# Second attention of a two-layer kernel: rotary sum ahead of the division, logits read inside the sum of gathered rows, row scaling behind the second gather

## Chip, cores and metric

The kernel runs on one core of one Trainium2 chip. The metric is the device time of one execution in microseconds (us), the median over several runs. The engines are called by the names of the profile: PE is TensorE's matmul side, PEld its weight loads, DVE is VectorE, ACT is ScalarE, POOL is GpSimd, SP is SyncE, which here only issues DMAs.

## What is computed

128 sequences of 64 tokens, 128 features, go through two layers. Each layer is an attention over a context and then a mixture of experts. The change lies in the attention of the second layer, which turns queries and keys by a position (rotary) before the scores:

```python
x = x + _L0_xattn_ref(_layernorm(x), ctx_1024, ctx_1024, mask, ...)
x = x + _L0_ffn_ref(_layernorm(x), ...)          # 32 experts, 4 per token
# second attention, 16 heads of 8
Q, K, V = query @ Wq + bq, key @ Wk + bk, value @ Wv + bv
Q = Q * cos + _rotate_half(Q) * sin
K = K * cos + _rotate_half(K) * sin
attn = softmax(Q K^T / sqrt(8));  context = attn @ V
x = x + context @ Wo + bo
x = x + _L1_ffn_ref(_layernorm(x), ...)          # 8 experts, 2 per token
```

The output of the first layer's experts is in DRAM, one row per token and expert. The second attention begins by gathering four rows per token and adding them to x.

## The kernel before

The residual X stays in SBUF. The program is a chain of stages: attention, slot table, experts, and the same again. Within a stage each engine has its own hand-written instruction list, and semaphores tie the lists together. There is no scheduler; the order of an engine's work is the order of the code.

The attention works in 32 rounds (ITERS), each on two tiles of 128 tokens. A round of an engine is software-pipelined: in round i it works on several pairs of tiles at different depths, and `on(k)` says whether pair i+k exists. For the second attention (`layer` = 1) the rounds are these.

- DVE, `body_with_sums`: the four row maxima of the scores of pair i (`score_unit`, L593); the division of the attention output of pair i-1 by its denominators (`divide`: reciprocal L633, product L635); the rotary step of pair i+1 (`weigh`, L641, twice for cos and twice for sin, the second behind semaphore `rot_psum`, then the sum L652, called `rotate`), which frees semaphore `rope`; the sum of the gathered rows of pair i+3 (`combine`: L571 and L573 fold four rows into one, L576 adds it to X); the copy of the router's logits of pair i-3 out of PSUM (`read_logits`, L608); statistics (L539); the addition of the projected output (`add_output`, L657); the choice of the experts (L621, L625); means and variances (L555, L561, L562), which free semaphore `offsets`.
- POOL, `body_with_gathers`: eight indirect DMAs (`gather`, L419, two tiles times four rows k = 0 to 3) for pair i+4, and `scale_both` (power L437, product L440), which turns the variances of the DVE round before into row scalings. `gather` for k = 0 waits for the first addition of `combine` two pairs earlier (semaphore `row_sum`), since the gathered rows lie in two buffers. `scale_both` waits for `offsets` and frees `scaled_both`.
- ACT, `body_with_spreads`: copies the transposed inputs (L828), places the values (L768), normalises rows with the scalings of `scale_both` (L787, L814), keeps the chosen experts (L752, L753), copies the maxima (L823), copies the transposed expert rows (L759), spreads keys over heads (L742, waits for `rope`), four exponentials (L725), spreads queries (L742).
- PE, `body_with_rotation`: scores (L907), values (L963) and denominators (L969) of pair i-1, four pairs of projections (L989, L990; the second two write the turned operands into bank M_), transposed maxima (L918), transposed scores (L932, L944), transposed expert rows of pair i-3 (L1019, waits for `rot`, since it writes bank M_), next values (L997), router (L1031), output projection (L1006, L1010, waits for the division and for the logits copy, since it writes the same bank), next inputs (L982, L984).

`hold` waits for a semaphore and puts a no-op behind the wait. In the loop the order of DVE is written out as

```python
if on(-1): divide(pv)
if on(1):  ... weigh(nx, QKe, P_, bq, bk, cos, "qk"); rotate(nx)
if on(3):  combine(i.at(3))
if on(-3): read_logits(p3)
```

Of the kernel before, what the change touches and what calls it, by code (L numbers as in the profile page):

```python
# [96 lines left out]
def hold(eng, sem, value):  # L97

    eng.wait_ge(sem, value)
    eng.nop(nofuse=True)  # L100


def build(nc, a, out, ts, ys, yt, bias_parts):

    with ExitStack() as ctx:
# [206 lines left out]
        def attention(layer):  # L312
# [32 lines left out]
            def tiles(buf, i):  # L345
                return buf[:, bass.ds(i.n * 2, 2), :]
# [20 lines left out]
            with nc.Block() as block:  # L367
# [43 lines left out]
                def _(pool):  # L411
                    def gather(i, k):

                        if k == 0 and i.n >= 2:

                            hold(pool, s["row_sum"], i.n * 2 - 3)
                        for j in range(2):
                            at, to = i.n * 2 + j, (j * K0 + k) * D
                            nc.gpsimd.indirect_dma_start(  # L419
                                out=gb[i.par][:, to:to + D], out_offset=None, in_=ys,  # L420
                                in_offset=bass.IndirectOffsetOnAxis(ap=slot[:, at, k:k + 1], axis=0),
                            ).then_inc(gathered[i.par], 16)
# [10 lines left out]
                    def scale_both(i, cols):  # L433

                        q = 1 - i.par
                        pool.wait_ge(s["offsets"], i.n + 4)
                        nc.gpsimd.tensor_tensor(small["rs"][q][:, cols], small["ve"][q][:, cols], power[:, cols], ALU.pow  # L437
                                                ).then_inc(s["rstd_both"], 1)
                        pool.wait_ge(s["rstd_both"], i.n + 4)
                        nc.gpsimd.tensor_tensor(small["mm"][q][:, cols], small["rs"][q][:, cols], small["nm"][q][:, cols],  # L440
                                                ALU.mult).then_inc(s["scaled_both"], 1)
# [61 lines left out]
                    def body_with_gathers(i, on):  # L503
                        if on(4):
                            gather(i.at(4), 0)
                        if (on(-2) or on(2)) and i.n > -2:
                            scale_both(i.at(-1), slice(0 if on(-2) else 2, 4 if on(2) else 2))
                        if on(4):
                            gather(i.at(4), 1)
                        if i.n == -3:  # L510
                            scale_both(i, slice(2, 4))
                        if on(4):
                            gather(i.at(4), 2)
                            gather(i.at(4), 3)
# [9 lines left out]
                def _(dve):  # L524
# [11 lines left out]
                    def tile_stats(i, st, done):  # L536

                        for j in range(2):
                            nc.vector.bn_stats(st[i.par][:, 6 * j:6 * j + 6],  # L539
                                               X[:, bass.ds(i.n * 2 + j, 1), :].rearrange("p i d -> p (i d)")  # L540
                                               ).then_inc(s[done], 1)
# [20 lines left out]
                        nc.vector.tensor_scalar(small["ve"][1 - q][:, cols], moments[:, cols, 1], EPS, None, ALU.add  # L562
                                                ).then_inc(s["offsets"], 1)

                    def combine(i):

                        q = i.par
                        hold(dve, gathered[q], (i.half + 1) * 16 * 2 * K0)
                        of = gb[q].rearrange("p (i h f) -> p i h f", i=2, h=2)
                        two = rows_sum.rearrange("p (i f) -> p i f", i=2)  # L570
                        nc.vector.tensor_tensor(two, of[:, :, 0, :], of[:, :, 1, :], ALU.add).then_inc(s["row_sum"], 1)  # L571
                        hold(dve, s["row_sum"], i.n * 2 + 1)
                        nc.vector.tensor_tensor(two[:, :, 0:D], two[:, :, 0:D], two[:, :, D:2 * D], ALU.add  # L573
                                                ).then_inc(s["row_sum"], 1)
                        hold(dve, s["row_sum"], i.n * 2 + 2)
                        nc.vector.tensor_tensor(tiles(X, i), tiles(X, i), two[:, :, 0:D], ALU.add  # L576
                                                ).then_inc(s["combined"], 1)
# [24 lines left out]
                    def read_logits(i):  # L602
                        dve.wait_ge(s["gate_psum"], i.g + 1)
                        src = R_[:, 2 * D:2 * D + 2 * n_e].rearrange("p (i e) -> p i e", i=2)
                        q = i.par
                        dst = lg[q][:, 0:2 * n_e].rearrange("p (i e) -> p i e", i=2)
                        if layer:
                            nc.vector.tensor_copy(dst, src).then_inc(s["logits"], 1)  # L608
                        else:
                            nc.vector.tensor_tensor(dst, src, gate_b[:].unsqueeze(1).broadcast_to([P, 2, E0]),  # L610
                                                    ALU.add).then_inc(s["logits"], 1)
# [17 lines left out]
                    def divide(i):  # L629

                        q = i.par
                        dve.wait_ge(s["o_psum"], i.g + 1)
                        nc.vector.reciprocal(rec, O_[:, 2 * D:4 * D]).then_inc(s["o_recip"], 1)  # L633
                        dve.wait_ge(s["o_recip"], i.g + 1)
                        nc.vector.tensor_tensor(aoT[q], O_[:, 0:2 * D], rec, ALU.mult).then_inc(s["o_normed"], 1)  # L635

                    def weigh(i, buf, src, b0, b1, tab, done):

                        for h, b in ((0, b0), (1, b1)):
                            at = slice(h * 2 * D, (h + 1) * 2 * D)  # L640
                            last = nc.vector.scalar_tensor_tensor(  # L641
                                buf[:, at].rearrange("p (b s) -> p b s", s=S),
                                src[:, at].rearrange("p (b s) -> p b s", s=S), b,
                                tab[:].unsqueeze(1).broadcast_to([P, 4, S]), ALU.add, ALU.mult)
                        last.then_inc(s[done], 1)

                    def rotate(i):

                        dve.wait_ge(s["rot_psum"], i.n + 1)
                        weigh(i, QKr, M_, bias_t[:, 4:5], bias_t[:, 5:6], sin, "rot")  # L650
                        dve.wait_ge(s["rot"], i.n + 1)
                        nc.vector.tensor_tensor(QKs[i.par], QKe, QKr, ALU.add).then_inc(s["rope"], 1)  # L652
# [33 lines left out]
                    def body_with_sums(i, on):  # L686
                        nx, pv, p3 = i.at(1), i.at(-1), i.at(-3)
                        if on(0):
                            for r in range(UNITS):
                                score_unit(i, r)  # L690
                        if on(-1):
                            divide(pv)
                        if on(1):
                            dve.wait_ge(s["qk_psum"], nx.g + 1)
                            if not (isinstance(nx.n, int) and nx.n < 1):

                                dve.wait_ge(s["rope"], nx.n)
                            weigh(nx, QKe, P_, bq, bk, cos, "qk")
                            rotate(nx)
                        if on(3):  # L700
                            combine(i.at(3))
                        if on(-3):
                            read_logits(p3)
                        if on(3):
                            hold(dve, s["combined"], i.at(3).n + 1)
                            tile_stats(i.at(3), small["st_a"], "stats_a")
                        if on(-1):
                            add_output(pv)
                        if on(-3):
                            choose(p3)  # L710
                        if on(-1):
                            hold(dve, s["added"], pv.g + 1)
                            tile_stats(pv, small["st_r"], "stats_r")
                        if on(3) or on(-1):
                            moments_of_both(i, on(-1), on(3))
# [820 lines left out]
        def gather(pool, n, XE, arrived):  # L1536
            R = len(XE)
            for c in range(GROUP):
                nc.gpsimd.indirect_dma_start(  # L1539
                    out=XE[n % R][:, c * ROW:(c + 1) * ROW], out_offset=None, in_=ts,  # L1540
                    in_offset=bass.IndirectOffsetOnAxis(ap=token_of_slot[:, n * GROUP + c:n * GROUP + c + 1], axis=0),
                ).then_inc(arrived[n % R], 16)
# [472 lines left out]
```

## Time and profile before

| what | value |
|---|---|
| runs | 1750.91, 1751.86, 1755.05 us, median 1751.86 |
| profiled execution | 1748.74 us, span 1746.9 us |
| granted TensorE clock, mean of the span | 0.92 |
| PE, DVE, ACT, POOL busy share | 79%, 67%, 55%, 62% |
| second attention | about 841 to 1294 us of the span |

The stage of the change is a quarter of the span. Its first score reduction starts at 880.53 us. A row of a timeline reads: start in us from the span's start, duration in us, engine, line, operation, output<-input, count of merged instructions, and in brackets the engine's idle time before it with what ended it. Lines are those of the kernel before. A granted clock of 1.00 is 2.4 GHz, 0.50 is 1.2 GHz.

### The profile page before, as it was taken

Reading aid. Unit: us, or ns where it says so; the run is one execution under the profiler, and the core shown is the slowest. Engines: PE = TensorE matmul, PEld = TensorE weight load, DVE = VectorE, ACT = ScalarE, POOL = GpSimd, SP = SyncE. Lnnn points to the kernel's source line nnn. Section 1 sums busy time; section 2 is a strip of 40 time slices with the busy share of each in tenths; the row PEclk is TensorE's granted clock in tenths of the full one; section 3 lists DMA queues with packets and bytes.
Section 4 is the critical chain, followed back from the end, with each engine's and each line's share of the span. In section 5 each row is a group of like instructions: output and inputs, shape, how many; then the busy total and the mean of one; then the engine's idle time right before and its main releaser. Section 6 shows DMA issues by size and latency. Waiting matters only on the chain. (4 is left out here: it accounts for less than half of the span.)

```text
span 1746.9 us, 56992 instructions
## 1 busy us (share of the span) xinstructions
PE 1372.5 (79%) x20302; PEld 1064.4 (61%) x20303; DVE 1176.1 (67%) x3431; ACT 957.2 (55%) x2418; POOL 1091.4 (62%) x1338
## 2 busy tenths in 40 slices
PE   5999999739677777777268888888854799999784
PEld 3677777514377767767156666666632578777663
DVE  5788888689577777777268888888869222322165
ACT  2677777617454545545067676777735344444332
POOL 3777777500377777776577777777210777777773
PEclk9999999959899999999688999999975899999987
DMA  4211111000144444443242222222100111111174
GB/s 161 89 45 36 45 36 46 21 7 1 26 109 105 108 103 109 106 106 104 64 158 66 63 63 62 61 63 59 33 14 1 51 54 55 54 54 54 55 231 136
DMA packets 136994, 122.85 MB, mean 70 GB/s; under 512 B 27675, under 2 KB 121915, under 8 KB 136123
## 3 DMA queue, kind: packets, MB, share of 16 engines
q0 software_dynamic: 26624, 56.35, 12.7%
q1 hardware_dynamic: 110078, 64.47, 12.1%
q8 instruction: 66, 1.08, 0.3%
q10 hardware_dynamic: 192, 0.67, 0.1%
q14 instruction: 34, 0.28, 0.1%
HBM read 80.24 MB, written 41.18 MB: 70 GB/s over the span
## 5 line engine op out<-in xcount | busy, mean ns | idle before, releaser
L1539 POOL DMA_INDIRECT arena<-expert_rows,token_of_slot x432 | 416.0, 963 | 283.8 <-issue 221.9
L419 POOL DMA_INDIRECT arena<-slot_results,slot x256 | 250.3, 978 | 95.7 <-issue 73.6
L1930 DVE TENSOR_TENSOR arena<-bank,arena 128x352 f32<-128x352 f32 x144 | 75.5, 524 | 222.6 <-ACT arena L1909 222.6
L1863 PE MATMUL bank<-W,arena 128*128 x576 | 198.7, 469 | 0.9 <-ACT arena L1921 0.9
L593 DVE TENSOR_REDUCE mx<-bank 128x8 f32<-128x512 f32 x256 | 158.4, 681 | 33.1 <-PE bank L907 31.9
L1774 POOL DMA_INDIRECT token_results<-arena,slot x144 | 141.2, 980 | 53.3 <-issue 43.7
L445 POOL TENSOR_TENSOR arena<-arena,fixed 128x1024 f32<-128x1024 f32 x64 | 121.3, 1916 | 44.6 <-ACT arena L733 44.6
L725 ACT ACTIVATE arena<-bank 128x512 f32<-128x512 f32 x256 | 131.3, 598 | 25.0 <-PE bank L944 25.0
L1637 PE MATMUL bank<-arena 128*128 128x128 f32 x1152 | 144.0, 279 | 0.0
L1877 PEld LDWEIGHTS bank<-W,arena 128*128 128x128 f32 (+1 forms) x864 | 115.5, 192 | 38.2 <-issue 30.8
L1637 PEld LDWEIGHTS bank<-arena 128*128 128x128 f32 x1152 | 136.9, 195 | 0.2
L1582 PE MATMUL bank<-fixed,arena 128*128 128x128 f32 x288 | 48.0, 290 | 101.9 <-DMA arena<-expert_rows,token_of_slot 101.9
L1877 PE MATMUL bank<-W,arena 128*128 (+1 forms) x864 | 121.5, 277 | 1.8 <-ACT arena L1916 1.8
L1863 PEld LDWEIGHTS bank<-W,arena 128*128 128x128 f32 x576 | 100.3, 194 | 33.4 <-issue 3.8
L1732 DVE TENSOR_SCALAR arena<-bank,arena 128x128 f32<-128x128 f32 x288 | 99.0, 344 | 30.7 <-PE bank L1637 30.5
L1909 ACT ACTIVATE arena<-bank 128x352 f32<-128x352 f32 x144 | 66.7, 463 | 94.9 <-PE bank L1863 94.9
L1467 PE MATMUL bank<-arena 128*128 128x288 f16 (+1 forms) x384 | 86.1, 394 | 39.7 <-DVE arena L1406 21.3
L633 DVE RECIPROCAL arena<-bank 128x256 f32<-128x256 f32 x64 | 111.9, 1749 | 4.3 <-PE bank L969 4.0
L742 ACT ACTIVATE arena<-arena,fixed 128x256 f32<-128x256 f32 x256 | 108.8, 508 | 4.2 <-DVE arena L652 4.2
L907 PE MATMUL bank<-arena 32*64 32x256 f32 x2048 | 83.7, 439 | 32.6 <-ACT arena L725 32.1
L1693 ACT ACTIVATE arena<-bank,fixed 128x512 f32<-128x512 f32 x72 | 49.5, 687 | 107.4 <-PE bank L1582 107.4
L1915 ACT ACTIVATE arena<-bank 128x256 f32<-128x256 f32 x144 | 55.2, 383 | 90.5 <-PE bank L1888 90.5
(220 smaller groups left out, 3379.0 us busy)
## 6 DMA issues: line engine op xcount, KB each, us to landing
slot_results<-arena SPq DMA_DIRECT2D x72, 256.0 KB, 2.4
arena<-in_ctx SPq DMA_DIRECT2D x64, 128.0 KB
expert_rows<-arena SPq DMA_DIRECT2D x64, 128.0 KB
arena<-token_results SPq DMA_DIRECT2D x32, 256.0 KB, 3.8
arena<-expert_rows,token_of_slot POOLq DMA_INDIRECT x432, 2.6
W<-in_w SPq DMA_DIRECT2D x4, 1032.0 KB, 5.1
X<-in_x SPq DMA_DIRECT2D x32, 128.0 KB, 2.2
arena<-slot_results,slot POOLq DMA_INDIRECT x256
```

The source lines that it names most:

```text
L419: nc.gpsimd.indirect_dma_start(out=gb[i.par][:, to:to + D], out_offset=None, in_=ys, in_offset=bass.IndirectOffsetOnAxis(ap=slot[:, at, k: ...
L445: nc.gpsimd.tensor_tensor(dst[i.par].rearrange("p (b j k) -> p b j k", b=4, j=4), src[i.par].rearrange("p (b k) -> p b k", b=4).unsqueeze( ...
L593: nc.vector.tensor_reduce(mx[:].rearrange("p (w c) -> p w c", w=2)[:, :, 32 * r:32 * r + 4], U_[r][:, :].rearrange("p (w j k) -> p w j k", ...
L633: nc.vector.reciprocal(rec, O_[:, 2 * D:4 * D]).then_inc(s["o_recip"], 1)
L725: nc.scalar.activation(Pt[r], U_[r][:, :], ACT.Exp, scale=SCALE).then_inc(s["probs"], 1)
L742: last = nc.scalar.activation(dst[i.par].rearrange("p (b j k) -> p b j k", b=4, j=4)[:, :, j, :], src[i.par].rearrange("p (b k) -> p b k", ...
L1539: nc.gpsimd.indirect_dma_start(out=XE[n % R][:, c * ROW:(c + 1) * ROW], out_offset=None, in_=ts, in_offset=bass.IndirectOffsetOnAxis(ap=to ...
L1637: last = nc.tensor.matmul(H_[2 * i.par + half][:, at:at + P], Wc[i.par][:, c * W1_0 + u * F0:c * W1_0 + (u + 1) * F0], XT[i.par][:, c * P: ...
L1732: nc.vector.tensor_scalar(GL[i.par][:, at], h[:, c, 0, :], Wc[i.par][:, b:b + 1], LIMIT, ALU.add, ALU.min)
L1774: nc.gpsimd.indirect_dma_start(out=yt[half], out_offset=bass.IndirectOffsetOnAxis(ap=row_of_slot[:, at:at + 1], axis=0), in_=YE[n % 4][:, ...
L1863: last = nc.tensor.matmul(H_[2 * r + u][:, 0:F1], XT[i.par][:, c * P:(c + 1) * P], W1a[:, bass.ds(x_e, 1), u * F1:(u + 1) * F1], start=Tru ...
L1877: last = nc.tensor.matmul(Y_[j.par][:, d * P:(d + 1) * P], AT[d % 2][0:f, k * P:(k + 1) * P], W1b[0:f, bass.ds(x_e, 1), k * P:(k + 1) * P] ...
```

## The change

Three edits, all in the second attention. On DVE the rotary step of the next pair goes ahead of the division of the last. In `combine` the copy of the logits goes between the second and the third addition; it is still done by itself where there is nothing to combine. On POOL the gather for k = 1 goes ahead of `scale_both`. What is computed stays the same, and so does the number of instructions.

```diff
@@ -503,10 +503,10 @@
                     def body_with_gathers(i, on):
                         if on(4):
                             gather(i.at(4), 0)
+                        if on(4):
+                            gather(i.at(4), 1)
                         if (on(-2) or on(2)) and i.n > -2:
                             scale_both(i.at(-1), slice(0 if on(-2) else 2, 4 if on(2) else 2))
-                        if on(4):
-                            gather(i.at(4), 1)
                         if i.n == -3:
                             scale_both(i, slice(2, 4))
                         if on(4):
@@ -562,7 +562,7 @@
                         nc.vector.tensor_scalar(small["ve"][1 - q][:, cols], moments[:, cols, 1], EPS, None, ALU.add
                                                 ).then_inc(s["offsets"], 1)
 
-                    def combine(i):
+                    def combine(i, logits_of):
 
                         q = i.par
                         hold(dve, gathered[q], (i.half + 1) * 16 * 2 * K0)
@@ -572,6 +572,8 @@
                         hold(dve, s["row_sum"], i.n * 2 + 1)
                         nc.vector.tensor_tensor(two[:, :, 0:D], two[:, :, 0:D], two[:, :, D:2 * D], ALU.add
                                                 ).then_inc(s["row_sum"], 1)
+                        if logits_of is not None:
+                            read_logits(logits_of)
                         hold(dve, s["row_sum"], i.n * 2 + 2)
                         nc.vector.tensor_tensor(tiles(X, i), tiles(X, i), two[:, :, 0:D], ALU.add
                                                 ).then_inc(s["combined"], 1)
@@ -688,8 +690,6 @@
                         if on(0):
                             for r in range(UNITS):
                                 score_unit(i, r)
-                        if on(-1):
-                            divide(pv)
                         if on(1):
                             dve.wait_ge(s["qk_psum"], nx.g + 1)
                             if not (isinstance(nx.n, int) and nx.n < 1):
@@ -697,9 +697,11 @@
                                 dve.wait_ge(s["rope"], nx.n)
                             weigh(nx, QKe, P_, bq, bk, cos, "qk")
                             rotate(nx)
+                        if on(-1):
+                            divide(pv)
                         if on(3):
-                            combine(i.at(3))
-                        if on(-3):
+                            combine(i.at(3), p3 if on(-3) else None)
+                        elif on(-3):
                             read_logits(p3)
                         if on(3):
                             hold(dve, s["combined"], i.at(3).n + 1)
```

DVE, inside the loop of the second attention, before: from the second half of the rotary step to the copy of the logits. The division stands ahead of all these rows. "L99" is the no-op of `hold` or its register.

```order
L641 SCALAR_TENSOR_TENSOR arena<-bank,fixed 128x256 [waits rot_psum]
L641 SCALAR_TENSOR_TENSOR arena<-bank,fixed 128x256
L652 TENSOR_TENSOR arena<-arena 128x512 [waits rot]
L99 ISA
L571 TENSOR_TENSOR arena<-arena 128x512 [waits gathered1]
L99 ISA
L573 TENSOR_TENSOR arena<-arena 128x2x128 [waits row_sum]
L99 REGISTER_ALU
L576 ISA [waits row_sum]
L576 TENSOR_TENSOR X<-X,arena 128x256
L603 REGISTER_ALU
L608 COPY arena<-bank 128x16 [waits gate_psum]
```

and now, with the changed file's line numbers (L635 and L637 are the division, L643 and L654 the rotary step, L578 the addition to X, L610 the copy of the logits), from the rotary sum on:

```order
L654 TENSOR_TENSOR arena<-arena 128x512 [waits rot]
L635 RECIPROCAL arena<-bank 128x256 [waits o_psum]
L637 TENSOR_TENSOR arena<-bank,arena 128x256 [waits o_recip]
L99 ISA
L571 TENSOR_TENSOR arena<-arena 128x512 [waits gathered1]
L99 ISA
L573 TENSOR_TENSOR arena<-arena 128x2x128 [waits row_sum]
L605 REGISTER_ALU
L610 COPY arena<-bank 128x16 [waits gate_psum]
L99 REGISTER_ALU
L578 ISA [waits row_sum]
L578 TENSOR_TENSOR X<-X,arena 128x256
```

The division has moved from ahead of the rotary step to between the rotary sum and the first addition, and the copy of the logits from behind the addition to X to ahead of it.

POOL, the same stage, before: the first two rows are `scale_both`, then six gathers, then the two of k = 0 for the next pair.

```order
L437 TENSOR_TENSOR arena<-arena,power 128x4 [waits offsets]
L440 TENSOR_TENSOR arena<-arena 128x4 [waits rstd_both]
L419 DMA arena<-slot_results,slot 128x128 x6
L419 DMA arena<-slot_results,slot 128x128 [waits row_sum]
L419 DMA arena<-slot_results,slot 128x128
L437 TENSOR_TENSOR arena<-arena,power 128x4 [waits offsets]
```

and now

```order
L437 TENSOR_TENSOR arena<-arena,power 128x4 [waits offsets]
L440 TENSOR_TENSOR arena<-arena 128x4 [waits rstd_both]
L419 DMA arena<-slot_results,slot 128x128 x4
L419 DMA arena<-slot_results,slot 128x128 [waits row_sum]
L419 DMA arena<-slot_results,slot 128x128 x3
L437 TENSOR_TENSOR arena<-arena,power 128x4 [waits offsets]
```

Four gathers instead of six follow `scale_both`, and four instead of two stand between the wait for `row_sum` and the next `scale_both`.

## Rows read from the trace of the kernel before

**Rows 1.** Stretches, PE: from:to, length, busy (instructions), granted clock, DMA share, GB/s

```profile
919.61:1238.40 318.79, 267.18 (x5937) 0.93 0.23 62
1016.53:1028.56 12.03, 9.91 (x239) 1.00 0.24 65
1092.05:1105.39 13.34, 11.34 (x239) 0.87 0.23 62
1105.39:1117.79 12.40, 9.99 (x239) 1.00 0.23 60
1117.79:1130.67 12.88, 11.30 (x239) 0.87 0.23 64
1130.67:1143.16 12.49, 10.02 (x239) 1.00 0.20 59
```

**Rows 2.** Waits, 919.61 to 1238.40 us: total us, times, longest us

```profile
POOL arena L437 <- DVE arena L562: 25.6, 22, 1.8
...
PE bank L1006 <- DVE arena L608: 22.2, 25, 1.3
...
DVE X L657 <- PE bank L1010: 13.1, 25, 0.8
DVE mx L593 <- PE bank L907: 11.3, 19, 1.1
```

**Rows 3.** Timeline of DVE, one round, 1028.67 to 1041.09 us

```profile
1028.67 0.68 DVE L571 TENSOR_TENSOR arena<-arena 128x512 f32<-128x512 f32 x1
1029.46 0.42 DVE L573 TENSOR_TENSOR arena<-arena 128x256 f32<-128x256 f32 x1
1030.08 0.42 DVE L576 TENSOR_TENSOR X<-X,arena 128x256 f32 x1 [0.20 <-DVE arena L573]
...
1031.59 0.42 DVE L657 TENSOR_TENSOR X<-bank,X 128x256 f32 x1 [0.50 <-PE bank L1010]
...
1034.27 2.48 DVE L593 TENSOR_REDUCE mx<-bank 128x8 f32<-128x512 f32 x4 [0.30 <-issue]
1036.67 1.75 DVE L633 RECIPROCAL arena<-bank 128x256 f32<-128x256 f32 x1
...
1038.79 1.65 DVE L641 SCALAR_TENSOR_TENSOR arena<-bank,fixed 128x256 f32<-128x256 f32 x4
1040.48 0.69 DVE L652 TENSOR_TENSOR arena<-arena 128x512 f32<-128x512 f32 x1
1041.09 0.68 DVE L571 TENSOR_TENSOR arena<-arena 128x512 f32<-128x512 f32 x1
```

**Rows 4.** Timeline of PE, the same round

```profile
1032.62 1.12 PE L907 MATMUL bank<-arena 32*64 32x256 f32 x32 [0.81 <-ACT arena L725]
...
1037.05 0.59 PE L990 MATMUL bank<-arena,Wm 128*128 128x256 f32 x2
...
1038.97 1.08 PE L944 MATMUL bank<-arena,fixed 32*64 32x256 f32 x27
1040.57 0.43 PE L1019 MATMUL bank<-fixed,arena 128*128 128x128 f32 x2 [0.53 <-DVE arena L641]
```

**Rows 5.** Timeline of ACT, the same round

```profile
1028.56 0.38 ACT L759 ACTIVATE arena<-bank 128x256 f32<-128x256 f32 x1 [2.29 <-PE bank L1019]
...
1034.41 1.12 ACT L768 ACTIVATE Vp<-bank 64x128 f32<-64x128 f32 x4
1035.56 0.88 ACT L787 ACTIVATE arena<-X,arena 128x128 f32 x2
...
1037.22 0.20 ACT L753 ACTIVATE top_at<-arena 128x16 uint32 x1
1037.90 0.38 ACT L823 ACTIVATE arena<-bank 128x256 f32<-128x256 f32 x1 [0.48 <-PE bank L918]
1041.04 0.38 ACT L759 ACTIVATE arena<-bank 128x256 f32<-128x256 f32 x1 [2.76 <-PE bank L1019]
```

**Rows 6.** Timeline of POOL, the same round

```profile
1034.05 1.04 POOL L437 TENSOR_TENSOR arena<-arena,power 128x4 f32<-128x4 f32 x1 [0.73 <-DVE arena L562]
1035.17 0.20 POOL L440 TENSOR_TENSOR arena<-arena 128x4 f32<-128x4 f32 x1
...
1036.85 0.94 POOL L419 DMA_INDIRECT arena<-slot_results,slot  x1 [0.30 <-issue]
1038.10 0.94 POOL L419 DMA_INDIRECT arena<-slot_results,slot  x1 [0.30 <-issue]
...
1040.60 1.39 POOL L419 DMA_INDIRECT arena<-slot_results,slot  x1 [0.30 <-issue]
```

## The prediction

> **What bounds the kernel now.** I read the stretches first, then the waits of the stage, then one round on four engines. From the first steady score reduction at 919.61 us to 1238.40 us lie 25 rounds, so a round takes 318.79 / 25 = 12.75 us on average [rows 1]. Single rounds, cut at ACT's copy L759, are unequal: 12.03, 12.40 and 12.49 us with a granted clock of 1.00, 12.88 and 13.34 us with 0.87. The reader should see two costs in the 12.75: a round at full clock of about 12.4 us, and now and then a fall of TensorE's clock to half. In the four successive rounds of rows 1 it falls in two; (13.34 + 12.40 + 12.88 + 12.49) / 4 = 12.78, so these four stand for the stage.
>
> In a full-clock round DVE is the bound. From one first addition L571 at 1028.67 to the next at 1041.09 are 12.42 us, in which DVE is idle for 0.20 us ahead of L576, 0.50 us ahead of L657 and 0.30 us of issue ahead of the reductions [rows 3]. The 0.50 is no accident of one round: L657 waits for PE's L1010 in all 25, 13.1 us together, because PE's output projection (L1006) waits for DVE's own copy of the logits, 25 times, 22.2 us together [rows 2]. DVE thus waits for itself, by way of PE.
>
> Close behind is the ring of ACT and PE. From L759 at 1028.56 ACT runs without a pause to the end of L768 at 1035.53 [rows 5]. PE then projects, turns maxima and scores, and its last L944 ends at 1038.97 + 1.08 = 1040.05 [rows 4]. L759 could start 0.47 us after L1019 starts (1041.04 - 1040.57), at 1040.52. This ring takes 1040.52 - 1028.56 = 11.96 us. Here it took 12.48, since L1019 sat idle 0.53 us for the rotary product L641, which stands on DVE behind the 1.75 us reciprocal [rows 3, 4].
>
> **Logits inside the sum.** The copy moves ahead of L576. It falls into the gap between L573 and L576 that is 0.20 us idle, but the statistics behind L576 need its result and now have no copy in front to cover their wait; I count half of the 0.20 as gained, 0.10. The larger part is that PE gets its release about 0.6 us earlier: the copy starts right behind L573 (start 1029.46) and no longer behind L576 (start 1030.08) [rows 3]. So the 0.50 us ahead of L657 goes. DVE's round becomes 12.42 - 0.50 - 0.10 = 11.82 us. That needs the router's product in time. It hangs on L1019 and L759, so it would be late without the next edit.
>
> **Rotary ahead of division.** Reciprocal and product take 1.75 + about 0.37 = 2.12 us (1036.67 to 1038.79) [rows 3]. Nothing on DVE gets shorter. L641 can start 2.12 us earlier, but its sin half waits for the turned operands, which PE finishes at 1037.05 + 0.59 = 1037.64 [rows 4]. It then ends near 1037.7 + 0.82 = 1038.5 instead of 1040.44. L1019 no longer waits, and ACT and PE run at their 11.96 us. Queued behind the division are now the output projection, which waited for the logits anyway, and the values of the next round. The division ends near 1038.5 + 0.61 + 2.12 = 1041.2, where the first addition starts now; PE wants it for L1006 at about 1 us later. So I cost this at nothing. If the cover is gone, L1006 is late by what is missing.
>
> **Second gather ahead of the scaling.** POOL still issues eight gathers and two small operations. Its work is no bound: a gather comes every 1.25 us (1038.10 - 1036.85), `scale_both` blocks 1.32 us (1034.05 to 1035.37) and POOL idles ahead of it, 25.6 us in 22 rounds [rows 2, 6]. But two gathers more, 2.50 us, now stand between the release by L571 and the power. The chain from the end of L768, in the time of the round shown: turned operands 1037.64, sin half 0.82 + 0.05, sum 0.61, division 2.12, L571 0.68: 1041.92. POOL's release 0.2 (L440's end at 1035.37 to L787 at 1035.56 is such a release), four gathers 5.0, `scale_both` 1.32: 1048.4. ACT needs 1.86 from L787 to the end of L753 (1035.56 to 1037.42) and 0.1 + 0.38 + 0.1 for L823: 1050.85 [rows 5]. L944 takes 1.2 and L759 follows 0.47 later: 1052.5. From 1028.56 that spans two rounds: 24.0 us, 12.0 each. This lies within 0.1 us of the ring of 11.96, so with two chains alike I take 12.1 us for a full-clock round. Both bounds stay: 11.96 from below, 12.4 from above if the earlier L571 does not come through. In the third rival the gathers themselves get longer.
>
> At the start of the stage POOL's queue sets the pace, and the first scalings slip behind two gathers each: the first rounds start up to 2.5 us later. The gathers behind them are not delayed, since they were only exchanged, and the slip is no longer than the slack that the next rounds get from an earlier rotary step (2.12 us in the first). I take 0 with 0 to +2.5 us.
>
> **The clock.** It decides how much of the gain remains. TensorE at half clock makes a round 13.34 or 12.88 us [rows 1]. Between L1019 and the scores PE waits three times: for L759, for the logits and, 0.81 us, for the exponentials L725 [rows 4]. The 0.53 us ahead of L1019 goes and the wait for the logits gets shorter; the wait for the exponentials stays. I expect the longer kind (13.34, a fall at the scores) to stay, priced at its full 13.34 since PE itself is then the chain, and the shorter kind to become rare: one fall in four rounds. That is (13.34 + 3 x 12.1) / 4 = 12.41 us per round, 0.34 less than 12.75. Times 25: 8.5 us.
>
> The Trainium skill, page "TensorE: Matmul & The Clock Gate", section "HAM oscillation — how this bites in real kernels", ties falls to idle gaps much longer than these. By it there would be no falls here, before or after. The trace differs: the clock fell in two of four rounds with waits of about 1 us. What such a rule would make of the changed kernel is the first rival.
>
> **The rivals.**
> 1. The falls vanish: PE waits less, and in the round of 12.03 us it had none. Then 12.1 per round: 0.65 x 25 = 16 us less. For it: the idle times that go. Against: the exponentials' wait stays.
> 2. The falls keep their pattern, two in four: (13.34 + 12.1 + 12.8 + 12.1) / 4 = 12.59, 4 us less, within what can be told.
> 3. POOL becomes the bound. One gather took 1.39 us instead of 0.94, beside L652 and L571 on DVE [rows 3, 6]. If all four on the chain stretch by that 0.45, it is (24.0 + 1.8) / 2 = 12.9 per round, +4 us without falls; with one gather stretched, 12.2. In the middle, 12.5 and some falls, it is about +1 us. The Trainium skill, page "SBUF — State Buffer", section "SBUF: two separate sides", says that DVE operations with two SBUF inputs and POOL lock each other out for a whole instruction. That would apply to the gather that now meets L573 and to the power, if it met L652 or L571; the one stretched gather agrees with it.
> 4. Slower: the clock falls in every round. The place is PE's wait for the exponentials ahead of L907; a round of 12.1 us may put the same idle stretch ahead of every fall. Then each takes 13.34 us: 0.59 x 25 = +15 us. The point from which it decides: (12.75 - 12.1) / (13.34 - 12.1), a fall in more than half of the rounds. Before it is half of them, but a part of these are of the cheaper kind.
> 5. The edits do nothing, because ACT turns out to be held elsewhere: 0 us.
>
> **How the numbers follow.** The profiled execution took 1748.74 us, 3.1 us under the median of 1751.86. Forecast: 1748.74 - 8.5 = 1740.2 on its scale, 1743.4 on that of the median, which I give. The rivals on the median's scale: 1735.6, 1747.8, 1753, 1767, 1751.9. Chances: forecast 0.40, falls vanish 0.14, same pattern 0.20, POOL 0.12, every round 0.08, nothing 0.06. A measurement of this kernel can tell 0.3%, about 5.3 us, from no change. Faster by more than that is the forecast nearly whole, rival 1 and a third of rival 2: 0.59. Slower is rival 4 and a little of rival 3: 0.10. The rest, 0.31, is within. The range leaves out rival 4 and the edges: 1733.5, all falls gone and the ring at its 11.96, to 1754, POOL's case with the late start.
>
> **What would show it.** L657's idle time ahead should fall from 13.1 us to under 3; L1019 should no longer wait for DVE; L571 should follow the division, and the idle time of L437 should go while ACT waits up to 0.5 us for L440 ahead of L787. A full-clock round should measure 12.0 to 12.2 us. The rounds with a clock near 0.87 should drop from about half to about a quarter. The forecast is wrong if full-clock rounds stay at 12.4, if L944 waits for L823 by more than 0.3 us per round, or if falls are as many as before.

## The result and the profile after

The changed kernel takes 1748.44 us, the median of 21 runs (1740.72 to 1758.4), against 1754.41 us of the kernel before, also 21 runs (1748.78 to 1757.96). The ratio is 0.9971 with a 95% interval of 0.9958 to 0.9983: 0.3% faster, 5 us, where 8.5 were forecast from a sum that fails in three places. The runs of the changed kernel spread over 18 us, twice as far as those before.

The profiled execution took 1751.0 us, 2.6 us above its median, while the one shown before lay 5.7 us under the median of 21 runs. So the two profiles can't be subtracted as wholes: the stage is longer in the profile after. What can be compared is single rounds. The stretches of PE, cut at ACT's copy L761 (L759 before), are from:to, length, busy (instructions), granted clock, DMA share, GB/s. The first row is 24 rounds, the others one round each; they answer to [rows 1].

```profile
927.80:1236.41 308.61, 260.35 (x5690) 0.92 0.23 62
...
1045.38:1057.32 11.94, 9.93 (x239) 1.00 0.24 66
1057.32:1070.88 13.56, 11.66 (x239) 0.87 0.23 63
1108.34:1120.28 11.94, 10.00 (x239) 1.00 0.24 65
1186.72:1200.46 13.74, 10.29 (x239) 1.00 0.17 48
```

The same 24 rounds before:

```profile
926.31:1233.00 306.69, 257.16 (x5690) 0.93 0.23 62
```

Full-clock rounds are 11.88 to 12.05 us in this execution: 9 of the 24. A round with a fall of the clock takes 12.8 to 13.8 us, 13.36 on average, and there are 14 of them. Before, the 24 rounds held 13 falls at 13.13 us on average and 11 full-clock rounds of 12.36. The last row is a third kind that I had not foreseen: 13.74 us at full clock.

Two falls of this execution, each with the stretch of its round ahead of it. The first two rows belong to round 11 (13.56 us), the last two to round 16 (12.84 us):

```profile
1057.32:1061.30 3.98, 2.16 (x17) 1.00 0.13 35
1062.00:1064.60 2.60, 2.60 (x84) 0.50 0.36 101
1120.28:1122.90 2.62, 1.37 (x12) 1.00 0.19 52
1123.20:1126.20 3.00, 2.60 (x37) 0.50 0.29 87
```

In round 11 PE waits 1.16 us for the logits and 0.62 us for the exponentials, and the clock falls as the scores begin. In round 16 it falls directly behind the wait for the logits (1.04 us). Of the 14 falls, 12 begin 3.7 to 4.5 us behind the round's L761, as in round 11, and cost more (13.14 to 13.77 us per round); two begin 2.9 us behind it and cost less (12.84 and 12.85). Before, the same count is 8 of the dearer kind (13.16 to 13.34) and 5 of the cheaper (12.79 to 12.94).

The waits of the stage after, 919.80 to 1241.83 us (who waited for whom, total us, times, longest us), answer to [rows 2]. L1008 is L1006 of before, L816 is L814, L909 is L907. L573 stands where the code waits for the first addition, L571: the gather starts 0.77 to 0.78 us after the end of L571 in all 22 rounds that wait.

```profile
POOL arena L419 <- DVE arena L573: 36.0, 21, 2.7
...
PE bank L1008 <- DVE arena L610: 25.9, 25, 1.4
ACT arena L816 <- POOL arena L440: 23.9, 25, 2.7
...
DVE arena L643 <- PE bank L992: 20.2, 19, 1.8
PE bank L909 <- ACT arena L727: 18.2, 25, 1.5
```

DVE's wait for the output projection (L659, 13.1 us before) is not among this stretch's waits any more, and POOL no longer waits ahead of L437. In their place DVE waits for PE's turned operands (L643 for L992, in 19 rounds), and ACT waits for POOL's scaling in every round, about 1 us each. PE still waits twice per round, for the logits and for the exponentials, in sum about as long as before (25.9 and 18.2 us in 25 rounds, 22.2 and 20.0 before).

One full-clock round on DVE, after; it answers to [rows 3]:

```profile
1053.73 1.74 DVE L643 SCALAR_TENSOR_TENSOR arena<-bank,fixed 128x256 f32<-128x256 f32 x4 [0.44 <-PE bank L992]
1055.51 0.69 DVE L654 TENSOR_TENSOR arena<-arena 128x512 f32<-128x512 f32 x1
1056.12 1.75 DVE L635 RECIPROCAL arena<-bank 128x256 f32<-128x256 f32 x1
1057.90 0.42 DVE L637 TENSOR_TENSOR arena<-bank,arena 128x256 f32<-128x256 f32 x1
1058.24 0.68 DVE L571 TENSOR_TENSOR arena<-arena 128x512 f32<-128x512 f32 x1
1059.02 0.42 DVE L573 TENSOR_TENSOR arena<-arena 128x256 f32<-128x256 f32 x1
1059.37 0.17 DVE L610 COPY arena<-bank 128x16 f32<-128x16 f32 x1
1059.64 0.42 DVE L578 TENSOR_TENSOR X<-X,arena 128x256 f32 x1
...
1060.57 0.41 DVE L659 TENSOR_TENSOR X<-bank,X 128x256 f32 x1
```

The copy of the logits L610 lies in the former gap ahead of the addition to X, and L659 starts without a wait.

The third kind of round shows on POOL and ACT. Timeline of POOL after, with its start, duration, and the idle time in brackets:

```profile
1189.12 1.20 POOL L419 DMA_INDIRECT arena<-slot_results,slot  x1 [2.67 <-DVE arena L573]
1192.32 0.94 POOL L419 DMA_INDIRECT arena<-slot_results,slot  x1 [2.00 <-issue]
...
1195.78 1.05 POOL L437 TENSOR_TENSOR arena<-arena,power 128x4 f32<-128x4 f32 x1
```

and of ACT and PE in the same round, which wait for it:

```profile
1197.29 0.88 ACT L816 ACTIVATE arena<-X,arena 128x128 f32 x2 [2.69 <-POOL arena L440]
```

```profile
1198.93 1.12 PE L946 MATMUL bank<-arena,fixed 32*64 32x256 f32 x32 [1.55 <-ACT arena L825]
```

Between two gathers POOL pauses 2.00 us for nothing that the profile shows. The kernel before has the pause too, in round 7 and again 14 rounds later. In all 14 traces of this study it lies in the same two places, ahead of the 114th and of the 226th of the stage's 256 gathers, and lasts 1.99 to 2.26 us. In the kernel before it falls into time in which POOL would otherwise have waited for L562, and L437 then follows without a wait:

```profile
1186.84 0.94 POOL L419 DMA_INDIRECT arena<-slot_results,slot  x1 [2.15 <-issue]
1187.80 1.05 POOL L437 TENSOR_TENSOR arena<-arena,power 128x4 f32<-128x4 f32 x1
```

### The profile page after: what moved, and what is told of

Read it like the earlier page. It is cut to its first block and busy times, and to the rows that moved or that the text cites. A ratio compares the mean times of both kernels' runs of the same rounds, so it can differ in the third digit from the quotient of the medians.

```text
span 1749.2 us, 56990 instructions
## 1 busy us (share of the span) xinstructions
PE 1371.7 (78%) x20300; PEld 1065.1 (61%) x20303; DVE 1177.3 (67%) x3431; ACT 960.5 (55%) x2418; POOL 1091.1 (62%) x1338
## 3 DMA queue, kind: packets, MB, share of 16 engines
q1 hardware_dynamic: 110078, 64.47, 12.1%
## 5 line engine op out<-in xcount | busy, mean ns | idle before, releaser
L1734 DVE TENSOR_SCALAR arena<-bank,arena 128x128 f32<-128x128 f32 x288 | 98.9, 343 | 30.2 <-PE bank L1639 28.2
L635 DVE RECIPROCAL arena<-bank 128x256 f32<-128x256 f32 x64 | 111.9, 1748 | 2.3 <-PE bank L971 2.2
L909 PE MATMUL bank<-arena 32*64 32x256 f32 x2048 | 83.6, 439 | 27.1 <-ACT arena L727 26.6
```

Of the source, the lines that this page charges most:

```text
L1734: nc.vector.tensor_scalar(GL[i.par][:, at], h[:, c, 0, :], Wc[i.par][:, b:b + 1], LIMIT, ALU.add, ALU.min)
```

## The experiments

Two theories. The clock theory: the edits shorten a full-clock round as forecast, and TensorE's clock, which falls in as many rounds as before or more, gives most of it back. The POOL theory: the gather ahead of the scaling delays ACT, at the start, in each round, or at the pause. Each kernel has its own runs of the kernel before beside it. "Falls" are the rounds, of 24 beginning with the first L759 (or L761) of the profile, whose granted clock is under 0.99, and "full-clock round" is the mean of the others.

**Each edit alone.** Rotary only:

```diff
-                        if on(-1):
-                            divide(pv)
                         if on(1):
...
                             rotate(nx)
+                        if on(-1):
+                            divide(pv)
```

> Only the rotary step ahead of the division; logits and gathers as before. Theory A (VectorE's own round, with its 0.50 us wait for PE's output projection, bounds a full-clock round, and the logits edit removes it): full-clock rounds stay near 12.4 us, at best 12.2, and the whole time stays within 3 us of the kernel before. Theory B (the division ahead of the rotary step is the bound): full-clock rounds fall to 12.0 and the time to within 2 us of the changed kernel.

Measured: 1762.67 us, ratio 1.0056 (1.0043 to 1.0069): slower by 10 us. Neither theory had that. The clock falls in 20 of 24 rounds, and the four others take 12.05 us. PE's waits (920 to 1240 us):

```profile
PE bank L1006 <- DVE arena L608: 43.1, 24, 2.1
...
PE bank L907 <- ACT arena L725: 0.7, 1, 0.7
```

The rotary step lets PE run ahead, but the copy of the logits now stands behind the division too, so PE waits 1.8 us per round for it instead of 0.9. In exchange the wait for the exponentials is gone (0.7 us instead of 19.0 in 24 rounds), and PE's waits in sum are as long as before: 46.3 us in 24 rounds against 47.1. So it is not more idle time that brings the extra falls; one long wait per round stands in place of two short ones. By the full-clock round alone theory A was wrong: with the rotary edit the rounds reach 12.05 without the logits edit.

Logits only: the copy as in the change, rotary step and POOL as before.

> Only the copy of the logits moved into the sum; rotary step behind the division, scaling ahead of the gather for k = 1. Theory A: the copy now comes about 0.6 us earlier, but the router's product on PE still hangs on the late rotary step, so VectorE waits for it instead: full-clock rounds 12.0 to 12.3 us. Theory B: nothing moves, 12.4 us, same time as before.

Measured: 1751.03 us, ratio 0.9999 (0.9983 to 1.0016). Full-clock rounds 12.02 us, as theory A had it; 12 falls, at 13.58 us. The shorter round and the dearer fall cancel. Here the waits move the other way (24 rounds):

```profile
PE bank L909 <- ACT arena L727: 35.6, 24, 1.5
PE bank L1008 <- DVE arena L610: 7.4, 24, 0.7
```

Each DVE edit alone brings the full-clock round to 12.0 us, so the prediction's "it would be late without the next edit" did not hold.

Gather only, the edit on POOL alone:

```diff
                             gather(i.at(4), 0)
+                        if on(4):
+                            gather(i.at(4), 1)
                         if (on(-2) or on(2)) and i.n > -2:
                             scale_both(i.at(-1), slice(0 if on(-2) else 2, 4 if on(2) else 2))
-                        if on(4):
-                            gather(i.at(4), 1)
```

> Only the gather for k = 1 ahead of the scaling. POOL theory (two gathers more ahead of the scaling delay ScalarE's rows): ScalarE waits for L440 in most rounds and the time rises by 3 to 8 us over the kernel before. Clock theory (the changed kernel lost its gain to falls of TensorE's clock alone): no change, within 2 us of before.

Measured: 1761.85 us, ratio 1.0051 (1.0038 to 1.0064), 17 falls. The POOL theory's sign is right and its size too small: 10 us. Four more falls come on top of the delay of ACT; how much of the 10 us is theirs was not separated. From the first gather to the first L759 this profile takes 90.06 us against 84.85 before: 5 us go at the start, and the 24 rounds take 311.89 us against 306.69, another 5.

**The change without the POOL edit.**

> The change without the POOL edit: rotary ahead of division and logits inside the sum. POOL theory: ScalarE no longer waits for L440 (26.9 us in 26 rounds of the changed kernel), rounds with a clock fall get 0.2 to 0.4 us shorter, and the kernel is 4 to 8 us faster than the changed one. Clock theory: ScalarE's wait was slack, time within 2 us of the changed kernel.

Measured: 1743.46 us (1733.15 to 1746.96), ratio 0.9959 (0.9945 to 0.9972): 5.0 us faster than the changed kernel by the medians, but only 2.1 us by the ratios, since the kernel before took 1751.23 us beside this one and 1754.41 beside the changed one. The first figure is in the POOL theory's range, the second at the edge of the clock theory's. Its profiled execution is the fastest of its runs, 1733.15 us, and has 3 falls in 24 rounds:

```profile
926.39:1216.37 289.98, 242.93 (x5690) 0.98 0.25 65
```

With the clock nearly steady the 24 rounds take 290 us, where the kernel before and the changed one took 307 and 309. Of the same kernel another run takes 1746.96. So this pair can't separate the POOL edit from the clock; the kernels with a steady clock below can.

**The clock, taken out.** PE gets matmuls that only fill time, in bank M_ where the next transposes overwrite them: three inside `inputs` (where PE then waits for the exponentials), and in some kernels two more behind the router (where it waits for the logits).

```diff
+                    def filler(n):
+
+                        for _ in range(n):
+                            nc.tensor.matmul(M_[:, 2 * D:3 * D], wv, wv, start=True, stop=True)
...
+                        if layer:
+                            filler(3)
                         for w in range(2):
                             last = nc.tensor.transpose(M_[:, (2 + w) * P:(3 + w) * P],
...
                         if on(-3):
                             gate(p3)
+                        if on(-3) and on(2):
+                            filler(2)
```

The changed kernel with three:

> The changed kernel with three matmuls of 128 x 128 more in each round, inside the transposes of the next inputs, where PE then waits for the exponentials. Their product is overwritten. Clock theory (14 of 24 rounds of the changed kernel carry a clock fall at 13.4 us, full-clock rounds take 12.0): the falls vanish or become rare, rounds 12.0 to 12.2 us, stage shorter by 15 to 20 us than in the changed kernel. Rival (the long rounds are long for another reason and the clock only follows): the number of long rounds stays, and the time rises by up to 24 x 0.1 = 2 us.

Measured: 1736.51 us (1735.84 to 1737.64), ratio 0.9907 (0.9888 to 0.9925). One fall in 24 rounds; 12 us faster than the changed kernel with 144 matmul instructions more in these rounds. Five runs lie within 1.8 us, where 21 runs without filling spread over 18. In part the spread is the clock as well: of the 21 runs the fastest (1740.72 us) has a mean granted clock of 0.927, the slowest (1758.4) 0.915. But the other kernels without a fall in their profile spread by 1.8 to 7.0 us over 4 to 6 runs, so a steady clock does not remove it. The forecast of 15 to 20 us was high by what the two paused rounds keep (13.62 and 13.77 us at full clock).

The kernel before with three:

> The kernel before with the same three matmuls per round. Clock theory: its 13 falls of 24 rounds vanish, all rounds take the 12.4 us of VectorE, stage shorter by 8 to 10 us. Rival: no change. The difference to the changed kernel with the same filling is then what the edits are worth without the clock: 24 x 0.4 = 10 us by the clock theory.

Measured: 1752.42 us, ratio 0.9996 (0.9982 to 1.0009), still 13 falls. Here the clock theory's number fails: filling ahead of the exponentials isn't enough, so the clock does not hang on that wait alone. The wait for the exponentials is gone here too (1.7 us in 24 rounds), and the one for the logits is left. It is as long in this kernel as in the changed one with the same filling, this kernel's row first:

```profile
PE bank L1013 <- DVE arena L608: 21.9, 24, 1.3
```

```profile
PE bank L1015 <- DVE arena L610: 22.1, 24, 1.1
```

PE's waits in sum are 29.4 and 31.2 us in 24 rounds, and still one kernel has 13 falls and the other one.

The changed kernel with both fillings, and the kernel before with both:

> As the changed kernel with three matmuls, and two more behind the router, where PE waits for the copy of the logits. Clock theory: any falls left by the three are gone, rounds 12.0 us, stage 18 to 22 us shorter than in the changed kernel. Rival: time up by 1 to 3 us against the kernel with three.

> The kernel before with filling at both places. Filling at the exponentials alone left 13 falls in 24 rounds. If its longer waits for the logits and for the rotary product keep the clock falling, the falls now go: rounds of 12.4 us, time 1742 to 1745 us, and the edits without the clock are worth the difference to 1734.2 us (filling at both places in the changed kernel). If the falls stay at 13, filling does not keep the clock up there, and the clock theory lacks something.

Measured: 1734.19 us (ratio 0.9897, 0.9879 to 0.9916) and 1737.9 us (0.9923, 0.9908 to 0.9938). Neither has a fall. The 24 rounds of each, the changed kernel first:

```profile
926.34:1217.91 291.57, 269.46 (x5930) 1.00 0.24 65
```

```profile
925.89:1219.78 293.89, 268.68 (x5930) 1.00 0.23 65
```

This pair has no falls in it. Without them the kernel before takes 12.25 us per round, not 12.4: the profile has 12.03 and 12.48 in turn. The changed one takes 12.15, of which 13.67 and 13.76 are the two pauses. The three edits are worth 3.7 us by the medians. The two kernels ran at different times and on different chips; by their ratios to the kernel before beside each it is 4.6 us (0.9923 - 0.9897), and the 24 rounds of the profiles differ by 2.3. And the filling gains about the same in both kernels: 1751.3 (the runs of before beside it) to 1737.9 is 13.4 us, 1748.4 to 1734.2 is 14.2 (13 by the ratios).

The changed kernel with the filling at the logits alone:

> The changed kernel with two matmuls only behind the router, where PE waits for the copy of the logits; none ahead of the exponentials' wait. If the wait for the exponentials is the place that brings the clock down (as the prediction had it), about half of the rounds still carry a fall and the time is within 4 us of the changed kernel, far above the 1736.5 us of the filling at the exponentials. If the logits' wait counts as much, falls become as rare as there and the time is 1735 to 1739 us.

Measured: 1738.22 us (ratio 0.992, 0.9906 to 0.9934), no fall in 24 rounds; the first two take 12.98 and 13.25 us at full clock, for a reason that I did not follow. Either filling takes the falls out of the changed kernel (one and none left). In the kernel before the one at the exponentials takes out none and both together take out all; the one at the logits alone was not run there. So no single wait brings the clock down in the changed kernel. Nor is it the length of the waits in sum: this kernel has none with 37.5 us of PE waits in 24 rounds, the kernel before with three matmuls has 13 with 29.4. What decides whether the clock falls stays open, and so does whether the matmuls help because PE is busy in the waits or because they shift the rounds in time.

**The POOL edit, without the clock.** Without the edit, three matmuls and then both fillings:

> The change without the POOL edit, with the three matmuls. With the clock out of the way this shows the POOL edit alone. POOL theory: full-clock rounds 0.1 to 0.2 us shorter than with the edit, 2 to 4 us in all. If POOL's scaling ahead of six gathers is what holds the changed order, it is slower by as much. If neither, within 1 us.

> The change without the POOL edit, filling at both places. If the clock is out of the way with three matmuls already: within 1 us of 1730.6 us. If the last falls (one in 24 rounds, and a spread of runs up to 1739.6) go with the second filling: 1729 us with all runs within 2 us.

Measured: 1730.56 us (ratio 0.9887, 0.9863 to 0.9911) and 1729.04 us (0.9869, 0.9852 to 0.9887). The expectation of 2 to 4 us was low: the POOL edit costs 6.0 us with one filling (1736.51 - 1730.56, runs taken together) and 5.2 with both (1734.19 - 1729.04; 4.9 by the ratios, since these were taken apart). The 24 rounds with both fillings and without the edit:

```profile
924.09:1211.75 287.66, 267.84 (x5930) 1.00 0.24 66
```

287.66 against 291.57 are 3.9 us: the two paused rounds are 12.60 and 12.63 us instead of 13.67 and 13.76, which makes 2.2 (without the edit the pause costs about 0.7 us, with it about 1.7), and the other 22 are each about 0.08 us shorter, 1.7. From the first gather to the first L761 it takes 82.44 us instead of 85.08: 2.6 at the start (in the other pairs with and without the edit it is 2.4, 4.7 and 5.2). Together 6.5, of which the end of the stage gives back a little (430.51 against 436.16 us from the first gather to the last L761, 5.7).

The edit from the fourth round on only, to separate the start:

> The changed kernel with three matmuls at the exponentials, but the gather for k = 1 goes ahead of the scaling only from the fourth round on; before that the order is the old one. Start theory (the slip of the first scalings costs about 3 us): time 3 us under the 1736.5 us of the kernel with the exchange everywhere, first L761 near 925.5 instead of 928.6 us. Steady theory (the cost lies in the rounds where POOL pauses for 2 us, 13.6 and 13.8 us against 12.6 and 12.7): start unchanged in its effect, the time within 1 us of 1736.5.

Measured: 1738.37 us (1735.07 to 1738.82), no faster than with the edit everywhere. The paused rounds are unchanged, 13.64 and 13.71 us. Neither number held: the start theory had 3 us less, the steady theory a time within 1 us of 1736.5. In its profile the second reduction comes about 3 us sooner after the first gather (53.3 instead of 56.5 us), but at the first L763 0.5 us is left (86.77 against 87.25), and a fall follows. The switch itself puts two gathers ahead of a scaling at the fourth round, so this kernel may pay there what it saved; that is argued, not measured. What the start alone costs is not settled by it.

**A version that beats both** is thus the change without its POOL edit and with both fillings, 1729.04 us: 1.3% under the kernel before, of which the two DVE edits are 8.9 us (1737.9 - 1729.04) and the steady clock the rest.

| kernel | us | ratio to before beside it | falls of 24 | PE's waits, us | full-clock round, us |
|---|---|---|---|---|---|
| before | 1754.41 | 1 | 13 | 47.1 | 12.36 |
| changed | 1748.44 | 0.9971 | 14 | 46.6 | 12.16 with the pause |
| rotary only | 1762.67 | 1.0056 | 20 | 46.3 | 12.05 |
| logits only | 1751.03 | 0.9999 | 12 | 45.7 | 12.02 |
| gather only | 1761.85 | 1.0051 | 17 | 45.6 | 12.23 |
| changed, no gather edit | 1743.46 | 0.9959 | 3, in its fastest run | 45.4 | 11.91 |
| before, three | 1752.42 | 0.9996 | 13 | 29.4 | 12.27 |
| before, both fillings | 1737.9 | 0.9923 | 0 | 20.5 | 12.25 |
| changed, three | 1736.51 | 0.9907 | 1 | 31.2 | 12.14 |
| changed, both fillings | 1734.19 | 0.9897 | 0 | 19.2 | 12.15 |
| changed, filling at the logits | 1738.22 | 0.992 | 0 | 37.5 | 12.23 |
| gather edit from the fourth round, three | 1738.37 | 0.992 | 2 | 30.9 | 12.15 |
| no gather edit, three | 1730.56 | 0.9887 | 1 | 30.2 | 11.98 |
| no gather edit, both fillings | 1729.04 | 0.9869 | 0 | 17.6 | 11.99 |

The falls and the waits (all of PE's in the 24 rounds) are of one profiled execution, the times are medians. Times of different groups of runs are best compared by their ratios.

## Why the prediction was right and wrong

**Right.** The ring of ACT and PE at 11.96 us: full-clock rounds without a pause take 11.88 to 12.05 after, 11.98 on average (11.93 without the POOL edit, slightly under the ring). The wait ahead of L657 goes, the copy of the logits fills the gap ahead of the addition to X, L1019 no longer waits for DVE, DVE waits for the turned operands instead by 0.44 us in a full-clock round. The sign is right, and the measured 1748.44 lies in the range. The price of a fall, "priced at its full 13.34 since PE itself is then the chain", measured 13.36 as the mean of all 14. That the whole gain, 5 to 6 us, still came near the forecast is partly luck: the rarer falls, which carried about half of the 8.5 us (rival 2, without them, has 4), did not come.

**Wrong: the clock.** The step was "I expect the longer kind (13.34, a fall at the scores) to stay [...] and the shorter kind to become rare: one fall in four rounds." There were 14 in 24, by the prediction's own signs ("if falls are as many as before") enough to call it wrong. The shorter kind did become rare, two instead of five; the longer kind did not stay but rose from 8 to 12. The idle time ahead of L1019 did go. But the same step has "the wait for the logits gets shorter", and it got longer: 25.9 us in 25 rounds against 22.2. The term behind it was "PE gets its release about 0.6 us earlier". That counts from DVE's first addition, and the addition itself now comes later for PE, since the division stands ahead of it. Counted from the start of L759 or L761, L571 starts at 0.11 us before (1028.67 - 1028.56) and at 0.92 us after (1058.24 - 1057.32), and the copy ends at 2.03 us before (1030.42 + 0.17) and at 2.22 us after (1059.37 + 0.17). PE's wait in these rounds is 0.98 us before and 1.16 us after. The place was wrong as well: rival 4 put the falls on the wait for the exponentials, and filling at either wait takes them out of the changed kernel. That longer waits for the logits made the falls more is not shown: PE's waits in sum are the same, 47.1 and 46.6 us in 24 rounds. With 14 falls at the price of 13.36 this execution's 24 rounds are not faster than before (308.61 against 306.69 us). Of the cases, rival 2 (the falls keep their pattern, 4 us less) came nearest.

**Wrong: the full-clock round of before.** I took 12.42 us, one round, for what the kernel does at full clock. With the clock held steady its rounds are 12.03 and 12.48 in turn, 12.25 on average. That DVE's own round is the bound fits: in two successive rounds of that profile, from L571 to L571, it takes 12.42 and 12.10 us and waits 0.50 and 0.52 us ahead of L657, and the 0.30 us of issue ahead of the reductions is there in the first only. The row of 12.03 was in [rows 1], and I read it as an exception. The gain of a full-clock round was therefore at most 12.25 - 12.0 = 0.25 us, where I had 12.42 - 12.1 = 0.32.

**Wrong: the POOL edit at nothing.** The chain was worked out at 24.0 us for two rounds, within 0.1 us of the ring, and in most rounds that held: the edit adds 0.08 us per round. ACT waits about 1 us for L440 (ahead of L816), not the 0.5 that I allowed, and nearly all of it is slack. Part of the difference is the release, which the chain had at 0.2 us and which takes 0.77. What I did not see is POOL's own pause of 2.0 us, once in 14 rounds. Before, it lay in POOL's idle time; now there is none ahead of L437, and the edit lengthens the round by 1.1 us twice. The start was given as "0 with 0 to +2.5 us" and measured 2.6 with both fillings, 2.4 to 5.2 over all pairs. In sum the edit costs 5.2 to 6.0 us. The rival that POOL becomes the bound had the right place, but its mechanism, gathers stretched by DVE's additions, is not what the paused rounds show: there the time goes in the pause, and the first gather behind the release takes 1.20 us instead of 0.94, not all four of them 1.39.

**What the edits are worth.** Without falls, 8.9 us for the two DVE edits, less 5.2 for the one on POOL: 3.7 (4.6 by the ratios). That is less than the 5 to 6 us by which the changed kernel was measured faster as it stands; the difference lies within the intervals. Why the falls number 13 in one order and 20 in another stays open. In the six kernels without filling PE's waits in sum are 45.4 to 47.1 us in 24 rounds, while the falls number 3 to 20.

## What to carry to other kernels

When TensorE works in a round with several short waits, take the time of a round with and without a clock fall apart, count the falls, and price both; an edit that shortens waits elsewhere can leave them on PE, or only move them from one place to another. Matmuls put into such waits gained 10 to 14 us here; in the kernel before the three at the exponentials alone gained nothing. A steady clock makes the kernel's other edits measurable. When an operation moves ahead within one engine's list, count its new time on the clock of the engine that waits for it, with all the other edits in. And before work is put ahead of a queue's only slack, look for the longest pause of that queue: the idle time may be what hides it.

## What the runs showed of the hardware

- The granted clock fell from 1.00 to 0.50 (2.4 to 1.2 GHz) although PE's longest single wait in the 24 rounds is 1.25 us (before), 1.55 us (changed) or 2.09 us (rotary only). 14 falls of 24 rounds went to 1 with three more matmuls of 128 x 128 per round, placed where PE waited, and the time fell by 12 us although PE had more to do. The Trainium skill, page "TensorE: Matmul & The Clock Gate", section "HAM oscillation — how this bites in real kernels", ties such falls to longer gaps; the measurement decides.
- Neither the longest single wait nor their sum tells how often the clock falls: 13 falls with waits of 29.4 us in 24 rounds, none with 37.5 us, 12 to 20 with 45.6 to 47.1 us.
- Identical programs spread by 18 us over 21 runs of the changed kernel and over 12 runs with the logits edit alone, by 9 us over 21 runs of the kernel before, and by 1.8 to 7.0 us over 4 to 6 runs of the kernels without a fall in their profile.
- POOL paused for 1.99 to 2.26 us ahead of the 114th and the 226th of 256 indirect DMAs, 112 apart, in all 14 traces, whatever the order of its other work; most other gathers follow each other after 0.30 us. The traces do not show what it does in the pause.
